# A hybrid block of attention and experts on one core: where the experts' low half is subtracted, and what the routing logits wait for

## The reference, cut to what matters

```python
x = x + attn_a(layernorm(x))   # q, k, v projections, short conv, silu, l2norm, delta rule, Wo
x = x + ffn(layernorm(x))      # experts
x = x + attn_b(layernorm(x))   # linear attention, chunk after chunk
x = x + ffn(layernorm(x))

def ffn(x):                    # xt: tokens x 128
    probs = softmax(xt @ Wg)                 # Wg 128 x 8, the routing logits
    topw, topi = top_k(probs, 2)             # renormalised to a sum of 1
    h = relu(einsum('nd,edf->enf', xt, W1))  # 8 experts, 128 -> 256
    y = einsum('enf,efd->end', h, W2)        # 256 -> 128
    return einsum('ne,end->nd', combine, y)
```

## Time and profile before

| what | us |
|---|---|
| median of 3 runs | 980.86 (978.05 to 982.71) |
| the profiled execution, its own time | 981.93 |
| its span from the first to the last instruction | 980.1 |
| VectorE busy | 669.7 (68%) |
| TensorE matmuls busy | 770.3 (79%) |
| ScalarE busy | 524.6 (54%) |
| GpSimd busy | 395.6 (40%) |

### The profile page before, as it was taken

How to read it: one execution, slowest core, us unless ns; L and a number is a source line. 1 busy time by engine, 2 the same in 40 slices (tenths; PEclk the granted TensorE clock), 3 DMA queues, 4 the chain that set the end, 5 groups by cost and what they waited for, 6 DMA issues and landing times.

```text
span 980.1 us, 17203 instructions
## 1 busy us (share of the span) xinstructions
PE 770.3 (79%) x5736; PEld 634.5 (65%) x5736; DVE 669.7 (68%) x1476; ACT 524.6 (54%) x1409; POOL 395.6 (40%) x433
## 2 busy tenths in 40 slices
PE   2645156694967859576778899999999999999997
PEld 1424034573756748465666787878787878888786
DVE  1148989888898887989784548484848484747450
ACT  5573446485684846563344836363535353536355
POOL 1075969495876758787343101010101010101012
PEclk9776576797998969997678999999999999999999
DMA  4231121203022030210101000000000000000000
GB/s 147 64 76 47 34 77 35 76 2 100 23 57 63 0 110 0 79 33 11 44 1 44 22 1 23 2 22 0 21 0 12 9 10 11 0 21 1 12 12 12
DMA packets 48589, 32.17 MB, mean 33 GB/s; under 512 B 37664, under 2 KB 38944, under 8 KB 48288
## 3 DMA queue, kind: packets, MB, share of 16 engines
q1 hardware_dynamic: 48544, 31.61, 11.3%
HBM read 18.76 MB, written 12.85 MB: 32 GB/s over the span
## 4 chain that ended last, share of the span: by engine, by line
PE 50%; DVE 29%; ACT 8%; issue 8%; DMA 2%; POOL 1%; SPq 0%; DVEq 0%; ACTq 0%; POOLq 0%
PE bank L1032 16%; PE bank L1171 6%; PE bank L1010 4%; DVE u L1336 4%; PE bank L1012 4%; PE bank L945 4%; PE bank L1011 4%; DVE hist_mem L1603 4%; PE bank L1148 3%; DVE hist_mem L1344 3%; DVE hist_mem L1340 3%; DVE prod_mem L1331 2%; DVE x L1468 2%; PE bank L1183 2%; PE bank L980 1%
## 5 line engine op out<-in xcount | busy, mean ns | idle before, releaser
L1032 PE MATMUL bank<-w,hid 128*128 128x128 f32 x2048 | 268.2, 287 | 62.3 <-DVE x L1468 58.3
L1032 PEld LDWEIGHTS bank<-w,hid 128*128 128x128 f32 x2048 | 259.0, 202 | 77.5 <-issue 33.3
L533 POOL TENSOR_TENSOR x_odd<-x_odd,y_odd 128x512 f32<-128x512 f32 x48 | 63.1, 1315 | 431.3 <-ACT y_odd L732 431.3
L709 ACT ACTIVATE hid<-bank 128x512 f32<-128x512 f32 x256 | 143.8, 600 | 109.8 <-PE bank L1012 106.6
L1010 PE MATMUL bank<-xT_h,w_h 128*128 128x512 f32 x256 | 118.2, 462 | 4.0 <-ACT hid L709 2.6
L1012 PE MATMUL bank<-xT_h,w_l 128*128 128x512 f32 x256 | 103.9, 406 | 0.0
L1011 PE MATMUL bank<-xT_l,w_h 128*128 128x512 f32 x256 | 103.9, 406 | 0.0
L518 POOL TENSOR_TENSOR oq_mem<-hist_mem,q_t 128x384 f32<-128x384 f32 (+1 forms) x96 | 101.9, 1098 | 0.0
L1336 DVE TENSOR_REDUCE u<-prod_mem 128x32 f32<-128x288 f32 x128 | 86.4, 675 | 2.6
L1610 DVE TENSOR_TENSOR prod_mem<-bank,causal 128x1024 f32<-128x1024 f32 x32 | 39.2, 1225 | 54.9 <-PE bank L1148 53.8
L1010 PEld LDWEIGHTS bank<-xT_h,w_h 128*128 128x128 f32 x256 | 50.7, 198 | 32.8 <-issue 15.0
(11 more groups left out here) (164 smaller groups left out, 1453.3 us busy)
## 6 DMA issues: line engine op xcount, KB each, us to landing
s_qkv<-qkv SPq DMA_DIRECT2D x24, 256.0 KB, 3.4
pin<-s_qkv SPq DMA_DIRECT2D x16, 256.0 KB, 2.8
x_in<-in_x SPq DMA_DIRECT2D x8, 256.0 KB, 2.9
q_p<-s_qkv SPq DMA_DIRECT2D x8, 256.0 KB, 2.7
s_o<-o_p SPq DMA_DIRECT2D x8, 256.0 KB, 2.0
o_T<-s_o SPq DMA_DIRECT2D x8, 256.0 KB, 3.0
x_r<-in_x SPq DMA_DIRECT2D x8, 256.0 KB, 3.2
s_x<-x_odd SPq DMA_DIRECT2D x8, 256.0 KB, 2.3
```

The costliest lines, as they stand in the source:

```text
L709: nc.scalar.activation(hid[:, e % 2, f], bank[:, ZB + f, :], ACT.Relu).then_inc(hid_ready, 1)
L1032: last = nc.tensor.matmul(bank[:, y_bank(e, wide), tokens], hid[:, e % 2, f, tokens], w2[:, e, f], start=(f == 0), stop=(f == FC - 1))
```

## The change

In `step1` the subtraction at line 1448 takes its first operand from the PSUM bank `MB` instead of `xfT`. Since the routing logits are written over the first columns of that bank, `moe_route` in `step1` first waits for the subtraction as well (`xT_rest`). Queues keep their order. The passage and `step2` stay as they were.

```diff
-            def moe_route(n):
+            def moe_route(n, split=False):
                 pe.wait_ge(xfT_ready, n + 1)
+                if split:
+                    pe.wait_ge(xT_rest, n + 1)
                 for j in range(J):
...
                 if out:
-                    moe_route(o)
+                    moe_route(o, split=True)
                 if prep:
                     prep_norms(c)
...
-            def moe_split(n):
+            def moe_split(n, src=xfT):
 
                 dve.wait_ge(xT_ready, n + 1)
-                tt(xT_l[:], xfT[:], xT_h[:].bitcast(F32), ALU.subtract).then_inc(xT_rest, 1)
+                tt(xT_l[:], src[:], xT_h[:].bitcast(F32), ALU.subtract).then_inc(xT_rest, 1)
...
                     elif at == (14, 3):
-                        moe_split(o)
+                        moe_split(o, bank[:, MB, :])
```

## The result

The changed kernel takes 1015.83 us (median of 4 runs, 1015.25 to 1016.30) against 981.26 us before: the ratio is 1.0352, with a 95% interval of 1.0325 to 1.0379. That is 34.6 us more, where 38.7 were forecast; 1019.5 was the forecast time.

A forecast was written before the change was run, and what follows sets the result against it. VectorE's chain of blocks was taken to set the pace. 29.9 + 2.9 + 2.6 + 3.3 = 38.7 us on the profiled 981.9 gives 1020.6; the runs' median lies 1.1 lower, so 1019.5 us, range 1002 to 1028.

The forecast's parts named there:

- The part that helps: Seven step1 subtractions at line 1448: reading PSUM they take 0.69 us each, giving back 5.7 us of VectorE's time.
- The path to line 1303: Steps 1 to 5, subtraction start to line 1303 (later 1305): 9.95 us through logits, prep_norms and ScalarE's passes; +29.9 us.
- The low clock: TensorE after its pause of about 5.4 us: logits and prep_norms at 1.2 GHz, 1.87 + 3.75 us instead of 1.02 + 1.96.
- the rival with the full clock: TensorE keeps its full clock after the pause: 23.9 us more, 1004.8 us; chance 0.17.
- the two cases of the prediction: TensorE at the low clock after the pause, 1019.5 us, against TensorE at full clock, 1004.8 us.
- GpSimd's chain in steps 2 to 5: Expert 7 late behind prep_norms delays GpSimd's lines 533 to 526: 0.9 us in steps 3 to 5, 0.2 in step 2; 2.9 us.
- the slack of 0.58: Time in us by which GpSimd's chain ended before VectorE summed its result; taken off that chain's delay.
- The wait at line 1305: Old line 1303 on VectorE: waits about 6.5 us for line 667 in each of steps 1 to 5, 32 in all.
- Steps 6 and 7: No prep_norms there, but expert 7 stands behind the logits, delaying expert 0 and GpSimd's chain: +2.6 and +3.3 us.
- The freed operand: Rival "The freed port decides": subtraction 5.7 us shorter, the logits' wait hidden, 975.2 us, 0.6% faster; chance 0.02.
- the hold: Rival "The hold stays": the subtraction waits for GpSimd from PSUM too, its 5.7 us stay, 1025 us; chance 0.06.

The follow-up runs named there:

- the wait alone: Changed kernel with the subtraction reading xfT from SBUF again, only moe_route's wait kept: 1015.77 us, ratio 1.0375 to the kernel before; run again 1.0360.
- norms first: Changed kernel with prep_norms put ahead of the logits in TensorE's queue, expert 7 still behind them: 995.97 us, ratio 1.0168 to the kernel before.
- The filled pause: Changed kernel with expert 7's up products made four times over in steps 2 to 7: 1003.53 us, ratio 1.0252 to the kernel before.

## Why the prediction was right

**The part that helps.** Right in kind and size: 0.68 us each in place of 10.6 us for the seven. The run with the wait alone shows that the operand's place does it, and that with the order of the changed kernel the held time is worth at most a few microseconds (3.0 us at line 1371 of step 6, and no difference clear of noise in the total); without the wait it is worth 3 to 4 us (ratios 0.9970 and 0.9957).

**The path to line 1303.** 9.95 us forecast, 9.60 to 9.72 measured. The products of two lines overlap a little, which my sum of two durations did not take off. Five steps give 28.6 us where 29.9 were forecast. This is the core of the loss, and the run with norms first takes it out.

**The low clock.** Logits 1.84 us and norms 3.68 us after a pause of 5.49 us, forecast 1.87 and 3.75; the rival with the full clock, 1004.8 us, is out for the changed kernel. The filled pause shows that the pause causes it: with TensorE kept busy the logits took 1.03 us in each of steps 2 to 7 and about 10 us came back, of the 14.7 between the two cases of the prediction, the norms still running slow in three of four steps. Not all of the 10 us are the terms that the prediction priced, as said at that run. That bursts behind an idle stretch start at half rate is also what the Trainium skill says ("TensorE: Matmul & The Clock Gate", section "HAM oscillation — how this bites in real kernels"); the trace agrees in all seven steps of the changed kernel.

**GpSimd's chain in steps 2 to 5.** Here a term was wrong: 2.9 us forecast, and line 1371 waits 0.9 us in all in these steps (the 4.2 of its group less 1.91 and 1.38 in steps 6 and 7). I let expert 7 run partly at the low clock; it took 1.95 us (at 360.92 above), so line 533 came only 2.08 us behind line 1305 instead of 1.37, and the 0.7 us were about the slack of 0.58. The stretches from line 1305 to the next subtraction even became 1.1 us shorter in sum. The reason lies in the kernel before: in the changed one they are 55.5, 55.4 and 55.3 us after steps 2, 3 and 4, in the one before 56.7, 54.8 and 56.7. At least two different things made the longer ones. After step 2 line 1407, which has both inputs in SBUF, was held by a microsecond beside GpSimd's line 533:

```profile
224.62 1.42 DVE L1407 TENSOR_TENSOR beaten<-beaten,lower 128x256 f32<-128x256 f32 x1
```

The prediction named this line and took nothing for it; in the changed kernel all of its calls took 0.42 to 0.43 us. After step 4 VectorE waited longer for products of TensorE (3.70, 1.09 and 0.86 us instead of 2.91, 0.48 and 0.36), and the sixteen products of line 1032 behind line 980 took 2.46 us there instead of 1.95. This fits a low clock that lasts longer; it was not tested by itself.

**The wait at line 1305.** It was put at 6.5 us in each of steps 1 to 5, 32 in all. It is 5.1 to 5.2, 26.0 in all: VectorE first waits 1.0 us a step for the logits at line 1396, which the prediction did not name. The 32.3 of the group come out only with the 6.4 us of two earlier calls; that likeness is chance. The distance to line 1305, on which the sum rests, holds both waits.

**Steps 6 and 7.** +1.4 and +3.2 us between the subtractions, forecast 2.6 and 3.3; a second profile has +1.4 and +5.2. The waits of both steps:

```profile
479.69 3.76 PE L1034 MATMUL bank<-w,hid 128*128 128x128 f32 x16
...
486.86 1.24 DVE L1419 SCALAR_TENSOR_TENSOR pick<-rank,pexp 128x32 f32<-128x32 f32 x1 [1.28 <-ACT pexp L693]
...
495.05 0.82 DVE L1371 TENSOR_REDUCE o_p<-oq_mem 128x128 f32<-128x640 f32 x1 [1.91 <-POOL oq_mem L526]
...
544.47 1.25 DVE L1419 SCALAR_TENSOR_TENSOR pick<-rank,pexp 128x32 f32<-128x32 f32 x1 [4.50 <-ACT pexp L693]
...
553.88 0.83 DVE L1371 TENSOR_REDUCE o_p<-oq_mem 128x128 f32<-128x640 f32 x1 [1.38 <-POOL oq_mem L526]
```

After step 6 VectorE waits 1.28 us at line 1419 where it had not waited, which the prediction did not name, and 1.91 at line 1371 where it had waited 0.29, as it said. Expert 0's first product starts 5.94 us behind the subtraction instead of 3.38, so the 2.6 us are right there; but line 1371 comes only 1.6 us later (17.89 instead of 16.28). After step 7 the wait at line 1419 is 4.50 us instead of 2.24, as named, and 1.38 at line 1371 are new. The change in steps 6 and 7 alone cost 0.55% (0.31 to 0.80), 5.4 us, close to the 5.9 forecast for them; that interval takes in 3 to 8 us.

**After the last subtraction** 1.7 us more passed in the profiled run, 1.6 of it in its last 36 us, where the code is the same. The second profile has 0.1 there, and 2.0 more in step 7. I had nothing for either and leave them as scatter of single executions.

**The rivals.** The freed operand decided nothing while the wait stood, and the hold did not stay. The largest error of size was not in the changed kernel but in what I expected of the run with norms first, 3 to 10 us against 16: a late expert 7 also moves GpSimd's additions across VectorE's line 1419, which has both inputs in SBUF and took 0.95 us instead of 0.35 in step 4 (0.4 to 0.6 us more in each of four steps), and VectorE's later waits for TensorE came out long in every step. What makes them long was not tested.

## What to carry to other kernels

A wait put into an in-order queue is priced by what is queued behind it, not by the instruction that needs it: the same wait cost 34.6 us in front of the norms and expert 7, and about 5 us behind them. If the engine that now waits is TensorE, price what follows at its lower clock. And before a wait is bought for a better operand, ask which part of the operation needs it at all: here 480 of 512 columns did not, and cutting it there gave the gain without making the logits wait.

## What the runs showed of the hardware

A 128x512 subtraction with both inputs in SBUF took up to 3.51 us, until two GpSimd operations had ended; with one input in PSUM it took 0.68 to 0.69 us every time, and with 480 columns 0.65. Making six products three times more than needed shortened the changed kernel by about 10 us, and the logits behind the wait then ran at 2.4 GHz (1.03 us instead of 1.84). A 128x256 operation with both inputs in SBUF took 1.42 us beside a GpSimd addition and 0.42 otherwise.
